# A graph kernel of four layers: six tiles' second products moved behind the lists, own rows added after the neighbours, gathers without a bounds check, another order of tiles

## The reference

```python
# layer 0: mean over neighbours, two weights, a combining weight
agg = mask @ h / max(deg, 1)
out0 = relu(concat([h @ W_self + b_self, agg @ W_nb + b_nb]) @ W_comb + b_comb)
# layers 1, 2, 3: attention with 8, 4 and 1 heads; e masked where adj is 0
e = leaky_relu(f_src[:, None] + f_dst[None, :], 0.2)
out = softmax(e, axis=-1) @ (h @ W)          # layer 2: then elu; layer 3: projected after the sum
```

## Time and profile before

| | |
|---|---|
| median of three executions | 1230.43 us |
| profiled execution, its own time | 1234.04 us |
| its span | 1232.3 us |
| busy: PE / DVE / ACT / POOL | 902 / 876 / 395 / 691 us |
| granted clock of PE, mean | 0.877 of 2.4 GHz |
| DMA moved | 242.7 MB, 197 GB/s |

### The profile page before, as it was taken

One profiled execution on the slowest core, in us unless ns is written; L12 is line 12 of the kernel. 1 busy time (PEld: TensorE's weight loads), 2 busy tenths in 40 slices (PEclk: granted clock), 3 DMA queues, 4 the chain that ended last, 5 costly groups with the idle time before them and its releaser, 6 DMA issues.

```text
span 1232.3 us, 12159 instructions
## 1 busy us (share of the span) xinstructions
PE 902.2 (73%) x2804; PEld 489.0 (40%) x2804; DVE 875.6 (71%) x2811; ACT 394.9 (32%) x1200; POOL 690.8 (56%) x648
## 2 busy tenths in 40 slices
PE   3985979899347367774889999577988834747774
PEld 1432434344135255551555666234444322313332
DVE  3876789950178598845899998098999945656563
ACT  3553646642023133330223334134354430101110
POOL 4043323356377777707777730377777017777772
PEclk9988989999769789896899999788899966868888
DMA  9999869722578688826657741366677117646662
GB/s 360 364 342 382 316 250 331 243 74 78 181 231 250 174 258 264 254 105 181 191 165 209 204 130 44 99 181 174 196 208 217 46 52 185 174 135 182 185 181 86
DMA packets 81448, 242.74 MB, mean 197 GB/s; under 512 B 16932, under 2 KB 19396, under 8 KB 77276
## 3 DMA queue, kind: packets, MB, share of 16 engines
q0 software_dynamic: 47488, 144.09, 41.4%
q1 hardware_dynamic: 33882, 97.82, 21.6%
HBM read 203.00 MB, written 53.64 MB: 208 GB/s over the span
## 4 chain that ended last, share of the span: by engine, by line
DVE 34%; PE 22%; POOL 15%; DMA 14%; issue 11%; ACT 3%; POOLq 1%; SPq 1%; ACTq 0%
POOL arena L1082 10%; DVE arena L1381 9%; PE psum L638 6%; PE psum L703 5%; PE psum L679 4%; DVE arena L1314 3%; DMA arena<-T,arena 3%; DMA arena<-XV,arena 3%; PE psum L751 3%; DVE arena L1131 3%; DMA arena<-in_adj 3%; DVE arena L1193 2%; DMA arena<-in_L_gnn_a 2%; DVE arena L1283 2%; DVE arena L1134 2%
## 5 line engine op out<-in xcount | busy, mean ns | idle before, releaser
L1082 POOL DMA_INDIRECT arena<-T,arena x476 | 520.6, 1094 | 319.9 <-issue 179.0
L703 PE MATMUL psum<-arena,misc 128*128 128x512 f32 x426 | 229.2, 658 | 68.2 <-DVE arena L1381 47.3
L679 PE MATMUL psum<-arena 128*128 128x264 f32 (+1 forms) x832 | 222.8, 415 | 14.6 <-ACT arena L797 14.6
L638 PE MATMUL psum<-arena 128*128 128x512 f32 (+1 forms) x416 | 198.9, 621 | 31.0 <-ACT arena L809 18.3
L616 PE MATMUL psum<-misc,arena 128*128 128x128 f32 (+1 forms) x520 | 87.3, 294 | 158.7 <-ACT arena L781 97.3
L679 PEld LDWEIGHTS psum<-arena 128*128 128x128 f32 (+1 forms) x832 | 166.8, 205 | 85.7 <-ACT arena L797 31.9
L1381 DVE TENSOR_TENSOR arena<-arena 128x512 f32<-128x512 f32 x238 | 160.7, 686 | 1.8
L616 PEld LDWEIGHTS psum<-misc,arena 128*128 128x128 f32 (+1 forms) x520 | 64.7, 151 | 209.0 <-ACT arena L781 110.2
L703 PEld LDWEIGHTS psum<-arena,misc 128*128 128x128 f32 x426 | 81.1, 207 | 153.9 <-issue 103.9
L781 ACT ACTIVATE arena<-arena 128x512 f32<-128x512 f32 x104 | 84.2, 810 | 160.6 <-DVE arena L1290 151.4
L751 PE MATMUL psum<-arena 128*128 128x512 f32 (+1 forms) x208 | 118.2, 721 | 19.1 <-ACT arena L794 19.1
(11 more groups left out here) (138 smaller groups left out, 972.9 us busy)
## 6 DMA issues: line engine op xcount, KB each, us to landing
arena<-in_adj SPq DMA_DIRECT2D x25, 1663.5 KB, 8.6
T<-arena SPq DMA_DIRECT2D x75, 260.0 KB, 3.5
arena<-T,arena POOLq DMA_INDIRECT x476, 3.8
T<-arena SPq DMA_DIRECT2D x25, 256.0 KB, 3.5
XV<-arena SPq DMA_DIRECT2D x25, 256.0 KB, 3.0
PW<-arena POOLq DMA_DIRECT2D x5, 1024.0 KB, 8.5
arena<-in_x SPq DMA_DIRECT2D x1, 3072.0 KB, 18.5
XV<-arena SPq DMA_DIRECT2D x1, 3072.0 KB, 22.3
```

The source lines that it names most:

```text
L638: last = e.matmul(p_own[which][0:n, :], HT[t % 2][:, k, 0:n], W0[which][:, k, :], start=k == 0, stop=k == 3 and which == 0)
L679: last = e.matmul(p_wh[0:n, a, :], ht[:, k, 0:n], WL[l][:, k, a, :], start=k == 0, stop=k == 3)
L703: e.matmul(p_num[s % 3].rearrange("p (a o) -> p a o", a=2), ident, halves(GB[:, BASE[l, s] + of[n][0], :])[:, :, 0:HALF], start=n == 0, st ...
L1082: e.indirect_dma_start(GB[:, BASE[l, s] + k, 0:ROW], None, dr["T"][l], bass.IndirectOffsetOnAxis(ap=(IDP if l else IDX)[:, t, k:k + 1], ax ...
```

## The change

- **Scan.** The second own products of tiles 20 to 25 are taken out of `JOBS` and done by PE and ACT in a list `TAIL` behind it; the transposed h of these tiles waits in X's memory. The pace of `JOBS` is 32 parts in place of 34. The stores of T and XV rows get two staging buffers each (`WO`, `VO`). `keep_x` moves from steps 6, 7 and 8 to steps 10, 12 and 24.
- **Score weights.** `reduce` on DVE is gone; POOL halves each product with a tree of additions (2048 to 1024 to 512 ... columns). The inputs of all six are loaded ahead, and so are W2 and W3.
- **Lists.** POOL, not SP, reads the lists back, after the scatter. The clearing of the ring is gone. One small DVE instruction a tile (degree) is gone from the scan.
- **Gathers.** L1082's DMA has no bounds check. An empty slot points to a new row N+1 of each table, which is zero in layer 0 and holds scores of -1e30 in the others, so `NEGM`'s addition is gone too.
- **Layer 0.** The neighbours' rows are added in place (TENSOR_TENSOR), and the scaled sum is put on the XV row afterwards (`own_added`); XV is gathered later (`XV_AFTER`: first after the slots of step 3).
- **Mean row.** The next layer's first gather doesn't wait for it; only tile 25's does. `ORDER` now begins 24, 23, 22, 1, 21, 2, 20, 3, 19, 0 in place of 24, 1, 23, 2, 22, 3, 21, 4, 20, 0.

```diff
-ORDER = [t for pair in zip([24, 23, 22, 21, 20, 19, 18, 17, 16, 15, 14, 13], [1, 2, 3, 4, 0, 5, 6, 7, 8, 9, 10, 11]) for t in pair] + [12, 25]
+ORDER = [24, 23, 22] + [t for pair in zip([1, 2, 3, 0, 4, 5, 6, 7, 8, 9], [21, 20, 19, 18, 17, 16, 15, 14, 13, 12]) for t in pair] + [10, 11, 25]
+EARLY = 20
+FIRST_XV = 3
...
-    work = prep + [(1.95, ("own", t, which, part)) for t in range(NT) for which in range(2) for part in range(2)]
+    work = prep + [(1.95, ("own", t, which, part)) for t in range(NT) for which in range(2 if t < EARLY else 1) for part in range(2)]
+    TAIL = [("own", t, 1, part) for t in range(EARLY, NT) for part in range(2)]
...
-        JOBS[next(t for t in range(NT + 1) if t == NT or spent <= total * (t + 1) / 34)].append(job)
+        JOBS[next(t for t in range(NT + 1) if t == NT or spent <= total * (t + 1) / 32)].append(job)
...
-    REDUCES = {7: (1, 0), 9: (1, 1), 12: (2, 0), 14: (2, 1), 18: (3, 0), 20: (3, 1)}
+    KEEP = [10, 12, 24]
+    XV_AFTER = [max(s, FIRST_XV + (s + 1) // 2) for s in range(NT)]
+    FINISH = [max(a if a == s else a + 1 for s, a in enumerate(XV_AFTER[:n + 1])) for n in range(NT)]
...
# POOL: score weights
+            e.tensor_tensor(S2, S1, AB[n].unsqueeze(1).broadcast_to([P, 4, D]), ALU.mult).then_inc(S["scored"], 1)
+            e.wait_ge(S["scored"], n + 1)
+            part = S2.rearrange("p k (h o) -> p k h o", o=F)
+            while F > 2:
+                F //= 2
+                halved(e.tensor_tensor(part[:, :, :, 0:F], part[:, :, :, 0:F], part[:, :, :, F:2 * F], ALU.add))
+                halved.wait()
+            e.tensor_tensor(WE[...], part[:, :, :, 0], part[:, :, :, 1], ALU.add).then_inc(S["reduced"], 1)
...
-        e.memset(flat[:, 0:CLEAR], 0.0).then_inc(S["cleared"], 1)
-        e.memset(flat[:, CLEAR:], 0.0).then_inc(S["cleared"], 1)
+        e.wait_ge(S["listed"], 16 * NT)
+        e.dma_start(LR, dr["LIST"].rearrange("(p t) c -> p t c", t=NT)).then_inc(S["lists_in"], 16)
...
                 e.indirect_dma_start(GB[:, BASE[l, s] + k, 0:ROW], None, dr["T"][l],
-                                     bass.IndirectOffsetOnAxis(ap=(IDP if l else IDX)[:, t, k:k + 1], axis=0),
-                                     bounds_check=N, oob_is_err=False).then_inc(S[f"gather{s % 8}"], 16)
+                                     bass.IndirectOffsetOnAxis(ap=(IDP if l else IDX)[:, t, k:k + 1], axis=0)).then_inc(S[f"gather{s % 8}"], 16)
...
-            e.wait_ge(S["mean_out"], 16 * (l if l < 3 else 4))
             for s in range(NT + lag):
+                if ORDER[s:s + 1] == [NT - 1]:
+                    e.wait_ge(S["mean_out"], 16 * (l if l < 3 else 4))
...
# DVE, layer 0
-                    added(e.scalar_tensor_tensor(y, GB[:, base + k, 0:D], SHARE[:, t, k:k + 1], y if k else xv[:, 0:D], ALU.mult, ALU.add))
+                    added(e.tensor_tensor(GB[:, base, 0:D], GB[:, base, 0:D], GB[:, base + k, 0:D], ALU.add))
+            own(e.scalar_tensor_tensor(y, GB[:, BASE[0, s], 0:D], RDEG[:, t:t + 1], xv[:, 0:D], ALU.mult, ALU.add))
+            e.scalar_tensor_tensor(X[:, t, :], y, 0.0, xv[:, D:2 * D], ALU.max, ALU.add).then_inc(S["x_new"], 1)
...
# DVE, shifted
-            soft(e.tensor_tensor(u, u, NEGM[:, t, 0:n].unsqueeze(2).broadcast_to([P, n, NH]), ALU.add))
```

More of the change, by code:

```diff
@@ L383, in edges @@
     WO = [take(WIDE) for _ in range(2)]
-    VO = take(D)
+    VO = [take(D) for _ in range(2)]
     ring = at[0]
@@ L391, in edges @@
     S1, S2, PA, PB = (take(4 * D, ("p (k o) -> p k o", dict(k=4))) for _ in range(4))
-    CLEAR = at[0] - ring
     MARK = [take(NSEG * PART // 2, None, FP16) for _ in range(2)]
-    AB = WO[1][:, 0:D]
+    AB = [take(D) for _ in range(6)]
+    RAW2 = take(D)
     assert at[0] <= after
@@ L466, in wait_num_read, with ht_of, wait_ht_free, wait_out @@
             e.wait_ge(S["y"], s + 1)
+    def ht_of(m):
+        return HT[m % 2] if m < EARLY or m >= NT else X[:, SPARE[m - EARLY], :].rearrange("p (k i) -> p k i", k=4)
+    def wait_ht_free(e, m):
+        if m < EARLY:
+            if m >= 2:
+                e.wait_ge(S["own_self"], m - 1)
+        elif m < NT:
+            for g in range(2):
+                e.wait_ge(S[f"x_kept{g}"], 16)
+                e.wait_ge(S["ln0"], g + 1)
+        elif m < NT + 2:
+            e.wait_ge(S["own_self"], EARLY)
+        else:
+            e.wait_ge(S["proj"], m - 2 - NT + 1)
+    def wait_out(e, name, t):
+        e.wait_ge(S[f"{name}{t % 2}_0"], 16 * (t // 2 + 1))
+        if t == NT - 1:
+            e.wait_ge(S[f"{name}{t % 2}_1"], 16)
     def wait_products(e, m):
@@ L512, in keep_x, with store, wl @@
                 for a, b in pieces(t):
-                    e.dma_start(dr["XV"][t * P + a:t * P + b, D:2 * D], X[a:b, t, :]).then_inc(S["x_kept"], 16)
+                    e.dma_start(dr["XV"][t * P + a:t * P + b, D:2 * D], X[a:b, t, :]).then_inc(S[f"x_kept{k}"], 16)
+        def store(job):
+            if job[0] == "own" and job[3]:
+                u = job[1]
+                if job[2] == 0:
+                    e.wait_ge(S["own_row"], u + 1)
+                    start_pieces(e, f"tout{u % 2}", u, lambda a, b: dr["T"][0][u * P + a:u * P + b, 0:D], lambda a, b: WO[u % 2][a:b, 0:D])
+                else:
+                    e.wait_ge(S["v_row"], u + 1)
+                    start_pieces(e, f"vout{u % 2}", u, lambda a, b: dr["XV"][u * P + a:u * P + b, 0:D], lambda a, b: VO[u % 2][a:b, :])
+        def wl(i):
+            e.wait_ge(S[("own_nb", "own_self")[i]], NT)
+            e.wait_ge(S[f"pw{i}"], 16)
+            e.wait_ge(S[f"pw{i + 2}"], 16)
+            src = dr["PW"][i + 2].rearrange("p (k a o) -> p k a o", k=4, a=2)
+            for a in range(2):
+                e.dma_start(WL[i][:, :, a, 0:HALF], src[:, :, a, :]).then_inc(S[f"wl{i}"], 16)
         e.dma_start(g["brow"][0:1, 1, :], dr["b_comb"].rearrange("(a n) -> a n", a=1)).then_inc(S["bcomb"], 16)
@@ L584, in turn @@
         def turn(which):
-            src = S2 if which == 3 else PA
+            src = PA
             e.wait_ge(S["w3" if which == 3 else f"pa{which}"], 16)
@@ L637, in own @@
             for k in (2 * part, 2 * part + 1):
-                last = e.matmul(p_own[which][0:n, :], HT[t % 2][:, k, 0:n], W0[which][:, k, :], start=k == 0, stop=k == 3 and which == 0)
+                last = e.matmul(p_own[which][0:n, :], ht_of(t)[:, k, 0:n], W0[which][:, k, :], start=k == 0, stop=k == 3 and which == 0)
             if part and which == 0:
@@ L663, in tensor @@
         for job in JOBS[NT]:
+            do(job)
+        for job in TAIL:
             do(job)
@@ L901, in scalar @@
             last.then_inc(S["we"], 1)
+            for job in TAIL if l == 0 else []:
+                own(*job[1:])
         for r in range(1, NT + 4):
@@ L1256, in vector @@
         lists = LR[:, :, 0:NK]
[L1257 removed]
+        place(e.tensor_scalar(EMPTY, lists, 0.0, float(N + 2), ALU.is_equal, ALU.mult))
         place(e.tensor_copy(NID, LR[:, :, 17]))
@@ L1488, in program @@
         dr["LIST"] = scratch("LIST", [NT * P, LROW])
-        dr["T"] = [scratch(f"T{l}", [N + 1, ROW]) for l in range(4)]
+        dr["T"] = [scratch(f"T{l}", [N + 2, ROW]) for l in range(4)]
         words = 51160
```

218 lines of the change are left out of this document (109 added, 109 removed).

## The result

| | before | after |
|---|---|---|
| median | 1233.49 us (7 runs) | 1224.36 us (7 runs, 1222.06 to 1227.06) |
| span of the profiled execution | 1232.3 us | 1225.3 us |
| granted clock of PE, mean | 0.877 | 0.885 |
| DMA moved | 242.7 MB | 257.5 MB |

The ratio is 0.993, with a 95% interval of [0.9905, 0.9952]. The change gains 9 us. The forecast was 1156 us, 74 us under the 1230.43 that it started from, and the measured time lies above both of its ranges (1135 to 1180 for the case itself, 1095 to 1190 in all).

A forecast was written before the change was run, and what follows sets the result against it. The bound changes by stage: three near floors (DVE, DMA, PE) in the scan, POOL's gathers in layers 0 and 3, DVE in 1 and 2. 277 + 224.7 + 222.8 + 213.9 + 219.9 = 1158.3, median 1156 us; range 1095 to 1190.

The forecast's parts named there:

- so it stands for 3 us: Layer 0: POOL waits 3 us at the first XV gather for the six tiles' second products to be stored.
- layer 0 at 224.7: Layer 0's length: 227.2 + 3 - 2 - 3.5 = 224.7 us, if a gather costs what it cost.
- Rival (d): Scan and layer 0: DVE's locks lose 30 us, first XV gather stalls POOL for 15; 1190 us, chance 0.05.
- I take 7: Scan: POOL's tree additions hold up DVE by 7 us, bounds 0 and 30.
- The 3.94 us row: Scan, earlier trace: at 196.27 a DVE instruction on one column took 3.94 us beside POOL's L1015.
- The floor that I had at 221 us: Scan: DMA transfers, 0.85 x 259.5 = 221 us, taken as a floor near DVE's 224.6.
- rival (b): Scan: PE, ACT and DVE wait in turn, or trees come late; end at 250, whole 1178 us, chance 0.14.
- 49 in place of 66.6: Lists: first gather comes 49 us behind the scan's end instead of 66.6, at 277 us.
- The mean row's wait: Layer boundaries: first gather no longer waits for the mean row; gains 3.5 us behind layers 0 and 1, 5.9 behind layer 2.
- The mask: Layers 1 and 2: dropping it from DVE saves 26 x 0.17 = 4.5 us each.
- nothing in it shows per-index work on bounds: Gathers: reason for no gain from dropping the bounds check; 1.01 us is the same with slots full or half empty.
- Rival (c): Gathers: empty slots all read one DRAM row, served one by one; 1465 us, chance 0.06 with anything else that loses.

The follow-up runs named there:

- xv5: The changed kernel with five XV buffers in place of three; 1197.93 us, ratio 0.9702 to the kernel before.
- reducedve: early26 without POOL's tree; DVE reduces at tiles 10, 11, 13, 14, 18, 19, inputs loaded ahead; second chip, ratio 0.9715 to the kernel before.
- notree: early26 without POOL's halving additions, each score weight the sum of two columns only; second chip, ratio 0.9733 to the kernel before.
- early26: xv5 with the second products of all 26 tiles in the scan's job list and pace 34; 1189.80 us, ratio 0.964 to the kernel before.
- tile0late2: early26 with tile 0 at place 18 of the order, not tenth; 1178.70 us, ratio 0.9558 to the kernel before.
- orderback3: early26 with the kernel before's order of tiles; 1192.04 us, ratio 0.9672 to the kernel before.
- spread: early26 with empty slots pointing to the lane's own row, their masking left out; second chip, ratio 0.9707 to the kernel before, 0.9693 when repeated.

## Why the prediction was wrong

The span was forecast at 1158.3 us and is 1225.3. The 67 us lie as follows: the scan 13.9 (241.9 for 228), the lists 8.2 (57.2 for 49), layer 0 34.2, layer 1 7.3, layer 2 7.3, layer 3 -3.8.

The forecast took 259.5 us for the end of the scan in the kernel before, 1.9 us behind the end of DVE's last tile (257.6); counted from that end on both sides, the scan was off by 15.8 us and the lists by 6.3.

- **The step that failed most: "so it stands for 3 us", and with it layer 0 at 224.7.** I priced the first XV gather's wait (9.5 us, not 3) and gave the late XV row 2 us of gain. I did not carry the delay on to the buffers. The row is used a round later, so it is freed a round later, and three buffers are not enough for two rows in one round: four more waits of 34.1 us in all. Of the layer's 34.2 us too many, *xv5* gives 29.2 back. Rival (d) had this stall at 15 us as something that could go wrong, but as a longer single wait, not as a lockstep. What makes up the last 5 us stays open.
- **The scan, "I take 7".** DVE's small steps took 17.8 us more (42.0 less 24.2) in the changed kernel, where I took 7 of bounds from 0 to 30. The 3.94 us row was the right evidence and I set it too low. The Trainium skill, page "SBUF — State Buffer", section "Who interferes with whom", describes a port pair that VectorE and GpSimd lock against each other; *reducedve* bears that out, with the two-input steps at 275 and 199 ns without the tree and 582 and 573 ns beside it. But even without it the end would not have been 228: *notree* ends the scan at 233.4. The floor that I had at 221 us from the DMA share of the earlier trace rows was an average over the stretch; no kernel here ends the scan before 233, 12 us higher, and DVE's wait for ACT's marking grew where its own work shrank.
- **The scan's rival (b) "doesn't come down".** I gave it 0.14, at 250. With 241.9 the end lies between it and my forecast. What moved it most was not the trees but the pace of the jobs: 245.3 at 32 parts, 235.5 at 34. I had taken that edit at nothing. No run shows that it costs anything in the whole.
- **The lists, "49 in place of 66.6".** PE's tiles with a first product alone do not take half of 7.81 us but 4.9. The chain after, in three of them (start, length):

```profile
271.72 1.96 PE psum L683 x4
274.11 1.73 PE psum L683 x4
276.61 1.96 PE psum L683 x4
...
281.50 1.96 PE psum L683 x4
```

 Each product is 1.96 + 1.73 us (the second part at 274.11 for the first of them). Between the parts lie 0.43 us of transposes, and behind them 0.78 us until ACT has copied the product (L855). In the kernel before, the second product ran in that time. Six such tiles are 29.4 us where I had 23.4: six of the 8.2 us. And *early26* shows that the second products could have been done in the scan with no loss to the first gather.
- **Layers 1 and 2.** The mean row's wait held: forecast 3.5, 3.5 and 5.9 us at the three boundaries (12.9), found 1.8, 1.9 and 5.2 us there (8.9) and 10.5 in the whole. The mask was mis-sized: its group of 4.9 us is gone from layer 1, but DVE's busy time fell by 2.2 us only (190.69 to 188.49), since small instructions overlap in time with the next (in the kernel before one starts at 257.29 for 0.16 us, the next at 257.36). The term left out is tile 0: its wait grew from 2.1 to 6.2 us in layer 1 and from 3.7 to 8.2 in layer 2, because DVE now reaches it sooner (67.9 us behind layer 1's first gather, where it was 74.6) while its 15 slots still come at POOL's pace. *tile0late2* shows that this wait counts. The new order's own gain, forecast at 2 us a layer, is not shown either (*orderback3*).
- **The gathers.** I took no gain, with a bound of 36 us a layer. The gap stays, as I argued, and gathers stand 1.26 us from start to start where I had 1.31; the check itself has a price of 53 ns, which I argued away ("nothing in it shows per-index work on bounds"). The row showed only that the price does not depend on how full the slots are. The Trainium skill, page "DMA: Bandwidth & Descriptors", section "Where the ~2 µs actually goes", calls descriptor generation small and variable. It says nothing of a check; the runs show that the check adds a twentieth to the 0.95 us that a gather takes on POOL, and not how much of the 0.95 us is descriptor generation. The check is why layer 3 came out better than forecast, and its 14 to 17 us are more than the whole gain: with it the changed kernel lies 0.4% above the kernel before.
- **Rival (c), the hot row.** Gathers land in 4.59, 4.24, 4.21 and 4.01 us on the mean in layers 0 to 3 where they had 4.12, 3.93, 3.89 and 3.61, and DMA shares are 0.59 to 0.69. That is far from the 0.9 and the 6 us that I had named as its sign. *spread* shows no gain from taking the common row away, so the 0.3 to 0.4 us more (0.5 in layer 0) go rather with the 15 MB more that the queues move; no run shows that directly.

## What to carry to other kernels

When a change uses a buffer later, count the buffer's rounds anew: what was three tiles of slack may be none, and an in-order queue behind the wait turns one late buffer into a lockstep of two engines. And before work is put off from a stage, look whether the stage has room for it: here PE had the time anyway, and the deferred work came back as a wait in the next stage.

An engine relieved in a stage with three near floors wins only down to the next floor. A share over the whole stretch (0.85 of 259.5 us, here) puts that floor too low. The wait for the feed shows it only once the other engine is out of the way: ACT stood 17.1 us for the matrix in the kernel before and 43.9 in *early26*.

## What the runs showed of the hardware that I had not expected

- An indirect DMA's issue on POOL takes 1007 ns (median) with a bounds check and 953 without, valid indices in both. The 0.30 us ahead of each does not change.
- A two-input DVE step of 40 columns, 0.20 us by itself, lasts as long as the two-input POOL instruction that runs beside it: 3.86, 3.53 and 4.34 us beside products of 2048 columns (3.8 us) and 2.4 us beside additions of 1024 columns (2.36 us), all in the scan of *early26*. A one-input step (L1262 at 119.29 us) beside the next addition, of 512 columns, took 0.20 us as everywhere. Moving six reduces of 2.27 us to POOL cost DVE 8 to 19 us and spared it 13.6.
- A DVE instruction of 189 ns taken out of a chain of small ones saves some 85 ns of DVE's busy time (2.2 us over 26).
